# A third accumulating transfer per half, moved loads and a single Block in an attention and FFN kernel

## Chip, cores and metric

One core of one Trainium2 chip. The metric is the device time of one execution in microseconds (us): the median of several runs.

## What is computed

Eight batches of x (512 channels, 1024 positions) go through attention with 16 heads of 32 channels and a key mask, then through a quantised linear layer, and x is added. Cut to what matters:

```python
Q, K, V = proj(Wq), proj(Wk), proj(Wv)                 # einsum 'oc,bct->bto', then 16 heads of 32
att = einsum('bhqd,bhkd->bhqk', Q, K) / sqrt(32) + b
att = softmax(att * m + (1 - m) * NEG_INF)
y = einsum('bhqk,bhkd->bhqd', att, V)                  # back to [B, C, T]
q, in_scale = per_token_quant_int8(y)                  # absmax of a row / 127, rounded
out = einsum('bsk,nk->bsn', q, weight) * in_scale * w_scale + bias
return x + out.astype(float16)
```

## The kernel before

The work has two stages, each in a Block of its own, with a barrier between them.

`project` makes Q, K and V for one batch at a time. Each fp32 operand is split in a high and a low part that TensorE multiplies at its fast rate; the parts of Q and K go to memory (`qk_d`), V too (`v_d`). In the last batch the V products are mixed with the first score maxima of attention. There `w_raw` is the buffer of the raw weights, and `x_hi` and `x_lo` lie in the same memory as `k_stack` and `q_stack`.

`attend` runs 32 steps of four heads. A step has 64 units (`t`), two halves of 512 queries by 8 tiles of 128 keys by 4 heads. In each unit TensorE makes one score block, 128 keys by 512 queries, transposed (`scores`, L724), and half of a row maximum for a coming step (`next_max`, `row_max`, L128), which VectorE reduces (L137). ScalarE takes the exponential into one of eight tiles `probs[:, kt]` (`exps`, L832). At the end of each group of four units `weigh` (L751) adds the previous tile's product with V. Maxima go back into the operands as extra rows: turned on TensorE (L144), split by ScalarE and VectorE (L151, L157), and stored by SyncE (`store_max`, L165) at slot 23 for the second half of the step (units from 32), and at slot 55 for the first half of the next one. The row sums of the softmax are taken at slot 55 (half 0) and, in the next step, at slot 23 (half 1).

The row sum is made in three ways. GpSimd starts DMA transfers that add one whole tile of `probs` (1 MB) onto another (`begin_pair`, L998), two per half: tile 0 onto 1, and 2 onto 3. It adds tiles itself into `acc` (`add`, L1014): 4 and 1, then 3, 5, 6. TensorE adds the rest in `sum_rows`: tile 7 with L763, `acc` with L766. Each tile's slot is free for the next half's exponentials once its reader is through: `FREED` says which add, `READ_BY` which transfer; `exps` waits accordingly. Each engine's order is written out by hand in its `step`; `prev`, `main` and `ahead` say which of the three steps in work take part.

```python
PAIRS_OF_TILES = ((0, 1), (2, 3))
FIRST, ADDED = 4, (1, 3, 5, 6)
...
                for tile in range(first, TT):
                    for h in range(GH):
                        pe.matmul(buf[h * DH:(h + 1) * DH, 0:N], ones[:, :], probs[:, tile, h, :], start=(tile == first), stop=False)
                pe.wait_ge(acc_done, ADDS * halves_before(s, half) + adds)
```

The rest of a step belongs to the step before: GpSimd's `normalise` (L1033) and `finish` (L1039, L1042), VectorE's absmax and scales, the turn of the rounded rows (slot 47) and the product with the weights (`ffn`, L784, slot 51). ScalarE's queue issues the loads between its exponentials (`loads`): K rows at units 0 to 2, bias rows at 4 and 5, V at 8, Q rows at 24 to 26 and 38 to 40, the residual at 30. Row maxima of the next step begin at unit 20 and need its K, bias and Q rows.

Of the kernel before, what the change touches and what calls it, by code (L numbers as in the profile page):

```python
# [25 lines left out]
P = 128  # L26
# [24 lines left out]
PAIRS_OF_TILES = ((0, 1), (2, 3))  # L51
FIRST, ADDED = 4, (1, 3, 5, 6)
# [15 lines left out]
MAX_ROWS = 16 * 2  # L68

# [98 lines left out]
def project(nc, x, mask, wqT, wkT, wvT, qk_d, v_d, bias_d, cond_b, fw, wT, ws_rep, fb_rep, w_scale, f_bias,  # L168
            banks, ring, q_stack, k_stack, neg_max, max_hi, max_lo, ident, v_out, v_stored,
            stack_set, k_loaded, q1_loaded, q2_loaded, rowmax_done, neg_max_done,  # L170
            ident_set, maxT_done, max_hi_done, max_lo_done, max_rows):

    QHI, QLO, KHI, KLO = range(4)
    with ExitStack() as ctx:
        sb = lambda name, shape, dt: ctx.enter_context(nc.sbuf_tensor(name, shape, dt))
        sem = lambda name: ctx.enter_context(nc.semaphore(name))

        w_raw = sb("w_raw", [P, CT, C], F32)
# [25 lines left out]
        proj_done = sem("proj_done")  # L204
# [5 lines left out]
        v_done = sem("v_done")  # L210
        part_stored = [sem(f"part_stored{i}") for i in range(2)]
# [8 lines left out]
        fw_done = sem("fw_done")  # L220
# [5 lines left out]
        GROUPS = 3 * TT  # L226
        V_BANKS = (0, 1, 2)
# [3 lines left out]
        STAGES = 2 * CT  # L231
        block = ctx.enter_context(nc.Block())

        @block.sync
        def _(sp):
# [62 lines left out]
            sp.wait_ge(stack_set, 2)  # L298
            for k in range(3):
                load_q(sp, qk_d, q_stack, 0, 0, 0, k, q1_loaded)  # L300
            for k in range(3):
                load_k(sp, qk_d, k_stack, 0, 0, k, k_loaded)
            for part in range(2):
                load_bias(sp, bias_d, k_stack, 0, 0, part, k_loaded)
            for k in range(3):
                load_q(sp, qk_d, q_stack, 0, 0, 1, k, q2_loaded)
            batch(B - 1, 1, last=True)

            for i in range(2):
                sp.wait_ge(part_stored[i], 32 * B * STAGES // 2)  # L310

        @block.tensor
        def _(pe):
# [13 lines left out]
            def batch(b, par, last=False):  # L327
# [31 lines left out]
                if last:  # L359

                    pe.wait_ge(k_loaded[0], LOADS_K)
# [155 lines left out]
        def _(pool):  # L517
# [11 lines left out]
            def batch(b, par, last=False):  # L529
                if last:  # L530
                    pool.wait_ge(proj_done, GROUPS * b)
                    set_rows(nc, q_stack[0], k_stack[0], stack_set)
                else:
                    split_x(b + 1, 1 - par)
# [16 lines left out]
def attend(nc, x, qk_d, v_d, bias_d, fw, ws_rep, fb_rep, out,  # L551
           banks, ring, q_stack, k_stack, neg_max, max_hi, max_lo, ident, v_out, v_stored,
           stack_set, k_loaded, q1_loaded, q2_loaded, rowmax_done, neg_max_done,
           ident_set, maxT_done, max_hi_done, max_lo_done, max_rows):

    with ExitStack() as ctx:
        sb = lambda name, shape, dt: ctx.enter_context(nc.sbuf_tensor(name, shape, dt))
        sem = lambda name: ctx.enter_context(nc.semaphore(name))

        v_in = sb("v_in", [P, 2, TT, P], F32)  # L560
# [26 lines left out]
        v_loaded = [sem(f"v_loaded{i}") for i in range(2)]  # L587
# [35 lines left out]
        block = ctx.enter_context(nc.Block())  # L623
# [19 lines left out]
        def _(sp):  # L643
            sp.dma_start(v_in[:, 0, :, :], v_d[0]).then_inc(v_loaded[0], 16)

# [33 lines left out]
        def _(pe):  # L679
# [47 lines left out]
            def next_max(s, par, t):  # L727
# [3 lines left out]
                if t % 2 == 0:  # L731
                    if pair == 0:
# [22 lines left out]
            def sum_rows(s, half, buf):  # L755
# [4 lines left out]
                first, adds = (LAST_POOLED, LAST_POOLED - 1) if last else (max(ADDED) + 1, ADDS)  # L760
# [8 lines left out]
            def turn_q(s, buf):  # L769
                if isinstance(s, int) and s == 0:  # L770
                    pe.wait_ge(ident16_set, 1)
                pe.wait_ge(q_done, 2 * s + 2)
# [45 lines left out]
        def _(act):  # L818
# [34 lines left out]
            def loads(s, par, t, prev, ahead):  # L853
# [7 lines left out]
                if ahead and t == 8:  # L861
# [5 lines left out]
                if prev and t == 30:  # L867
                    load_res(s - 1)
                if s == 0 and t == 24:
                    act.wait_ge(stack_set, 4)  # L870
                if ahead and t in (24, 25, 26):
                    load_q(act, qk_d, q_stack, s + 1, 1 - par, 1, t - 24, q2_loaded)
# [27 lines left out]

            for s in range(STEPS + 1):
# [3 lines left out]
        def _(dve):  # L905
            nc.vector.memset(ones[:, :], 1.0).then_inc(const_set, 1)
# [47 lines left out]
            def step(s, par, prev=True, main=True, ahead=True):  # L954
                for t in range(UNITS):
# [30 lines left out]
        def _(pool):  # L986
            set_rows(nc, q_stack[1], k_stack[1], stack_set)
            nc.gpsimd.memset(ident16[:, :], 0.0).then_inc(zeroed, 1)
# [55 lines left out]
            def step(s, par, prev=True, main=True, ahead=True):  # L1044
                if prev and main:
                    add(s - 1, 1, 3)
                if prev:
                    normalise(s - 1, 0)
                if main:
                    for i in range(2):  # L1050
                        begin_pair(s, 0, i)
# [3 lines left out]
                if main:  # L1055
                    for k in range(1, 4):
                        add(s, 0, k)
                if main and ahead:
                    for i in range(2):
                        begin_pair(s, 1, i)  # L1060
# [13 lines left out]
def program(nc, x, mask, wqT, wkT, wvT, cond_b, wT, w_scale, f_bias, out):  # L1074
# [6 lines left out]
    with ExitStack() as ctx:  # L1081
# [9 lines left out]
        v_out = ctx.enter_context(nc.sbuf_tensor("v_out", [P, 2, C], F32))  # L1091
# [38 lines left out]
```

## Time and profile before

| | |
|---|---|
| time, median of 3 runs | 2441.13 us (2439.86 to 2441.28) |
| the profiled execution | 2436.68 us, its span 2434.8 us |
| TensorE matmul busy | 2381.2 us, 98% |
| GpSimd busy | 1673.1 us, 69% |
| VectorE busy | 1560.6 us, 64% |
| ScalarE busy | 1347.4 us, 55% |
| GpSimd's DMA queue (the accumulating transfers) | 132.13 MB, 27.4% of 16 engines' span |
| chain that ended last, TensorE's share | 64% |
| chain that ended last, the stores of `max_lo` | 5% |

Projection ends at about 556 us; from there to the end it is attention. In the tables of the profile a line such as L724 is a line of the kernel before, an arrow gives output and inputs, "idle before" is what the engine stood still ahead of an instruction and who ended that. PE is TensorE, ACT ScalarE, DVE VectorE, POOL GpSimd, SP SyncE; ACTq and SPq are issues of DMAs on their queues.

### The profile page before, as it was taken

Reading aid. Unit: us, or ns where it says so; the run is one execution under the profiler, and the core shown is the slowest. Engines: PE = TensorE matmul, PEld = TensorE weight load, DVE = VectorE, ACT = ScalarE, POOL = GpSimd, SP = SyncE. Lnnn points to the kernel's source line nnn. Section 1 sums busy time; section 2 is a strip of 40 time slices with the busy share of each in tenths; the row PEclk is TensorE's granted clock in tenths of the full one; section 3 lists DMA queues with packets and bytes.
Section 4 is the critical chain, followed back from the end, with each engine's and each line's share of the span. In section 5 each row is a group of like instructions: output and inputs, shape, how many; then the busy total and the mean of one; then the engine's idle time right before and its main releaser. Section 6 shows DMA issues by size and latency. Waiting matters only on the chain.

```text
span 2434.8 us, 37355 instructions
## 1 busy us (share of the span) xinstructions
PE 2381.2 (98%) x12344; PEld 1343.4 (55%) x12376; DVE 1560.6 (64%) x1683; ACT 1347.4 (55%) x2536; POOL 1673.1 (69%) x677
## 2 busy tenths in 40 slices
PE   8999999997999999999999999999999999999996
PEld 7888888884444444444444444444444444444442
DVE  3311111145777787777777777777777777777771
ACT  3322222214666666666666666666666666666664
POOL 3322223414788888888778888887888888888777
PEclk9999999998999999999999999999999999999999
DMA  6655555365677766776777776766776667766751
GB/s 242 255 193 205 211 195 196 149 211 131 149 160 159 159 148 153 161 158 154 156 158 160 156 161 152 159 148 154 158 161 156 153 151 160 159 155 152 157 111 46
DMA packets 143498, 396.55 MB, mean 163 GB/s; under 512 B 14584, under 2 KB 50424, under 8 KB 127296
## 3 DMA queue, kind: packets, MB, share of 16 engines
q0 software_dynamic: 18144, 132.13, 27.4%
q10 hardware_dynamic: 48864, 129.19, 22.0%
q1 hardware_dynamic: 76416, 134.34, 15.1%
q8 instruction: 34, 0.56, 0.1%
q14 instruction: 40, 0.33, 0.0%
HBM read 161.51 MB, written 100.93 MB: 108 GB/s over the span
## 4 chain that ended last, share of the span: by engine, by line
PE 64%; DMA 6%; issue 2%; DVE 2%; POOL 2%; SPq 0%; ACT 0%; ACTq 0%; POOLq 0%; DVEq 0%
PE score L724 21%; PE pv L751 18%; PE ring L128 17%; DMA q_stack<-max_lo 5%; PE ring L784 4%; PE ring L763 2%; PE ring L766 2%; DVE neg_max L137 1%; DMA k_stack<-bias_part 1%; PE ring L775 1%; POOL acc L1014 1%; DMA probs<-probs 0%; PE ring L144 0%; POOL acc L1026 0%; SPq L165 0%
## 5 line engine op out<-in xcount | busy, mean ns | idle before, releaser
L832 ACT ACTIVATE probs<-score 128x512 f32<-128x512 f32 x2048 | 1075.3, 604 | 583.2 <-PE score L724 570.3
L137 DVE TENSOR_REDUCE neg_max<-ring 128x1 f32<-128x1024 f32 x1024 | 1208.6, 1220 | 236.7 <-PE ring L128 225.1
L724 PE MATMUL score<-q_stack,k_stack 100*128 100x512 f32 x2048 | 875.4, 429 | 12.3 <-ACT probs L832 5.5
L1014 POOL TENSOR_TENSOR acc<-acc,probs 128x2048 f32<-128x2048 f32 x189 | 866.9, 4587 | 25.2 <-DMA probs<-probs 10.5
L128 PE MATMUL ring<-k_stack,q_stack 98*128 98x512 f32 x2048 | 810.6, 396 | 12.8 <-DMA k_stack<-bias_part 12.5
L724 PEld LDWEIGHTS score<-q_stack,k_stack 100*128 100x128 f32 x2048 | 387.4, 189 | 492.2 <-ACT probs L832 357.6
L751 PE MATMUL pv<-probs,v_in 128*32 128x512 f32 x4096 | 546.3, 605 | 0.0
L128 PEld LDWEIGHTS ring<-k_stack,q_stack 98*128 98x128 f32 x2048 | 390.7, 191 | 79.1 <-DMA k_stack<-bias_part 12.8
L1014 POOL TENSOR_TENSOR acc<-probs 128x2048 f32<-128x2048 f32 x63 | 289.0, 4588 | 105.0 <-DMA probs<-probs 105.0
L526 POOL TENSOR_TENSOR q_stack<-x_raw,k_stack 128x1024 fp32r<-128x1024 f32 x28 | 67.7, 2455 | 293.1 <-ACT k_stack L402 293.1
L998 POOL DMA_DIRECT2D probs<-probs x126 | 108.7, 863 | 170.2 <-PE pv L751 163.3
L751 PEld LDWEIGHTS pv<-probs,v_in 128*32 128x32 f32 x4096 | 80.6, 108 | 184.8 <-ACT probs L832 162.5
L475 DVE TENSOR_TENSOR part_lo<-score,part_hi 128x512 fp32r<-128x512 f32 x24 | 16.4, 691 | 179.3 <-ACT part_hi L427 179.2
L538 POOL TENSOR_TENSOR part_lo<-k_scaled,part_hi 128x512 fp32r<-128x512 f32 x64 | 82.4, 1307 | 55.1 <-ACT part_hi L430 55.1
L784 PE MATMUL ring<-fw,qT 128*128 128x512 bf16 x480 | 110.0, 382 | 6.2 <-issue 4.9
L1039 POOL TENSOR_TENSOR half<-prod,fb_rep 128x512 f16<-128x512 f32 x64 | 81.5, 1273 | 47.5 <-DVE prod L951 47.5
L325 PE MATMUL ring<-k_stack,w_hi 128*128 128x512 f32 x256 | 101.5, 396 | 0.0
L325 PE MATMUL ring<-q_stack,w_hi 128*128 128x512 f32 x256 | 101.3, 396 | 0.0
L325 PE MATMUL ring<-k_stack,w_lo 128*128 128x512 f32 x256 | 101.2, 395 | 0.0
L430 ACT ACTIVATE part_hi<-k_scaled 128x512 fp32r<-128x512 f32 x64 | 39.0, 628 | 112.1 <-DVE k_scaled L486 83.2
L914 DVE STREAM_TRANSPOSE sums_turned<-ring 128x512 f32<-128x512 f32 x64 | 45.9, 717 | 84.5 <-PE ring L766 84.5
L951 DVE SCALAR_TENSOR_TENSOR prod<-ring,scale,ws_rep 128x512 f32<-128x512 f32 x64 | 48.1, 751 | 80.4 <-PE ring L784 80.4
(101 smaller groups left out, 2028.9 us busy)
## 6 DMA issues: line engine op xcount, KB each, us to landing
probs<-probs POOLq DMA_DIRECT2D x126, 1024.0 KB, 8.0
q_stack<-qk_part ACTq DMA_DIRECT2D x183, 256.0 KB, 4.5
k_stack<-qk_part ACTq DMA_DIRECT2D x90, 512.0 KB
qk_part<-part_hi SPq DMA_DIRECT2D x64, 512.0 KB, 2.6
qk_part<-part_lo SPq DMA_DIRECT2D x64, 512.0 KB, 3.5
v_steps<-v_out SPq DMA_DIRECT2D x64, 256.0 KB, 2.2
v_out<-x ACTq DMA_DIRECT2D x32, 512.0 KB, 5.7
out<-v_out SPq DMA_DIRECT2D x64, 256.0 KB, 2.0
```

Of the source, the lines that this page charges most:

```text
L128: mm = pe.matmul(ring[:, half * N:(half + 1) * N], q_stack[par][0:ROW_MAX, chunk, h, qt * P:(qt + 1) * P], k_stack[par][0:ROW_MAX, h, half ...
L137: nc.vector.tensor_reduce(neg_max[:, pair // CHUNK, pair % CHUNK:pair % CHUNK + 1], ring[:, :], AX_X, ALU.max, negate=True).then_inc(neg_m ...
L325: return pe.matmul(bank[:, :], lhsT, rhs, start=(k == 0), stop=(k == 3 * CT - 1))
L526: nc.gpsimd.tensor_tensor(x_lo[par][:, a, :], x_raw[:, a, :], x_hi[par][:, a, :].bitcast(F32), ALU.subtract).then_inc(x_lo_done, 1)
L538: nc.gpsimd.tensor_tensor(part_lo[:, g % 2, th * N:(th + 1) * N], k_scaled[:, i % 2, :], part_hi[:, g % 2, th * N:(th + 1) * N].bitcast(F3 ...
L724: pe.matmul(score[score_bank(t)][:, :], k_stack[par][0:ROWS, h, kt * P:(kt + 1) * P], q_stack[par][0:ROWS, half, h, :], start=True, stop=T ...
L751: mm = pe.matmul(pv[h * DH:(h + 1) * DH, :], v_in[:, par, kt % TT, h * DH:(h + 1) * DH], probs[:, kt % RING, h, :], start=(kt % TT == 0), ...
L784: mm = pe.matmul(buf[:, cols], qT[:, tt, :], fw[:, tt, cols], start=(tt == 0), stop=(tt == TT - 1))
L832: nc.scalar.activation(probs[:, kt, h, :], score[score_bank(t)][:, :], ACT.Exp).then_inc(exp_done, 1)
L998: pool.dma_start(probs[:, b, :, :], probs[:, a, :, :], accum_op=ALU.add).then_inc(pair_done[i], 16)
L1014: nc.gpsimd.tensor_tensor(acc[:, half, :, :], first, probs[:, tile, :, :], ALU.add).then_inc(acc_done, 1)
L1039: nc.gpsimd.tensor_tensor(half16[:, half, :], prod[:, half, :], fb_rep[:, cols], ALU.add).then_inc(half_done, 1)
```

## The change

A third transfer per half adds tile 6 onto tile 5; GpSimd's adds take tiles 1, 3, 7, 5; `acc` then holds all eight tiles, and TensorE's sum has no term from `probs` except in the very last half. The third transfer waits for the weigh of tile 5 and the exponentials of tile 6. GpSimd's order of issues, adds and finishes is new. On ScalarE's queue V moves to unit 16, the residual to 22, the second half of Q to 33, 34 and 36. VectorE takes absmax of half 0 at slot 27. The two stages share one Block, with waits in place of the barrier; `v_in` lies outside the stages and serves as `w_raw` before; V of step 0 is loaded from the first stage; the constant rows 96 to 99 of the stacks are set alone (K first), and only the bias loads wait for them.

```diff
-PAIRS_OF_TILES = ((0, 1), (2, 3))
-FIRST, ADDED = 4, (1, 3, 5, 6)
+PAIRS_OF_TILES = ((0, 1), (2, 3), (6, 5))
+FIRST, ADDED = 4, (1, 3, 7, 5)
...
-    nc.gpsimd.memset(q_stack[:, :, :, :].bitcast(F32), LIFT).then_inc(stack_set, 1)
-    nc.gpsimd.memset(k_stack[:, :, :].bitcast(F32), 1.0).then_inc(stack_set, 1)
+    nc.gpsimd.memset(k_stack[ROW_BIAS:ROWS, :, :].bitcast(F32), 1.0).then_inc(stack_set, 1)
+    nc.gpsimd.memset(q_stack[ROW_BIAS:ROWS, :, :, :].bitcast(F32), LIFT).then_inc(stack_set, 1)
...
-        w_raw = sb("w_raw", [P, CT, C], F32)
+        w_raw = v_in[:, :, :, :].rearrange("p i a c -> p (i a c)").rearrange("p (a c) -> p a c", a=CT)
...
-        V_BANKS = (0, 1, 2)
+        V_BANKS = tuple((bank + SCORES - TT) % SCORES for bank in range(SCORES))
...
-            sp.wait_ge(stack_set, 2)
+            sp.wait_ge(proj_done, GROUPS * (B - 1))
             for k in range(3):
                 load_q(sp, qk_d, q_stack, 0, 0, 0, k, q1_loaded)
             for k in range(3):
                 load_k(sp, qk_d, k_stack, 0, 0, k, k_loaded)
+            sp.wait_ge(stack_set, 1)
             for part in range(2):
                 load_bias(sp, bias_d, k_stack, 0, 0, part, k_loaded)
             for k in range(3):
                 load_q(sp, qk_d, q_stack, 0, 0, 1, k, q2_loaded)
+            sp.wait_ge(fw_done, 1)
+            for i in range(2):
+                sp.wait_ge(v_stored[i], 16 * (B - 1) * TT // 2)
+            sp.dma_start(v_in[:, 0, :, :], v_d[0]).then_inc(v_loaded[0], 16)
             batch(B - 1, 1, last=True)
...
-        block = ctx.enter_context(nc.Block())
...
-            sp.wait_ge(stack_set, 4)
+            sp.wait_ge(proj_done, PROJECTED)
             for k in range(3):
                 load_q(sp, qk_d, q_stack, 1, 1, 0, k, q1_loaded)
             for k in range(3):
                 load_k(sp, qk_d, k_stack, 1, 1, k, k_loaded)
+            sp.wait_ge(stack_set, 3)
             for part in range(2):
                 load_bias(sp, bias_d, k_stack, 1, 1, part, k_loaded)
...
+                if isinstance(s, int) and s == 0 and t < SCORES:
+                    pe.wait_ge(v_done, B * TT - SCORES + 1 + t)
...
-                first, adds = (LAST_POOLED, LAST_POOLED - 1) if last else (max(ADDED) + 1, ADDS)
+                first, adds = (LAST_POOLED, LAST_POOLED - 1) if last else (TT, ADDS)
...
-                if ahead and t == 8:
+                if ahead and t == 16:
...
-                if prev and t == 30:
+                if prev and t == 22:
                     load_res(s - 1)
...
-                if ahead and t in (24, 25, 26):
-                    load_q(act, qk_d, q_stack, s + 1, 1 - par, 1, t - 24, q2_loaded)
+                if ahead and t in (33, 34, 36):
+                    load_q(act, qk_d, q_stack, s + 1, 1 - par, 1, (33, 34, 36).index(t), q2_loaded)
...
+            for i in range(2):
+                act.wait_ge(part_stored[i], 16 * B * STAGES)
...
-                    if t == 19 and prev:
-                        take_absmax(s - 1, 0)
-                        take_floor(s - 1)
...
                     if t == SUMS_1 + 4 and prev:
                         spread(s - 1, 1)
+                        take_absmax(s - 1, 0)
+                        take_floor(s - 1)
...
                 pool.wait_ge(pv_done, QH * TT * s + half * TT + b + 1)
+                if a > b:
+                    pool.wait_ge(exp_done, UNITS * s + GH * (half * TT + a + 1))
...
                 if prev and main:
+                    begin_pair(s, 0, 0)
                     add(s - 1, 1, 3)
+                elif main:
+                    begin_pair(s, 0, 0)
                 if prev:
                     normalise(s - 1, 0)
                 if main:
-                    for i in range(2):
-                        begin_pair(s, 0, i)
+                    begin_pair(s, 0, 1)
                     add(s, 0, 0)
                 if prev:
                     normalise(s - 1, 1)
                 if main:
+                    begin_pair(s, 0, 2)
                     for k in range(1, 4):
                         add(s, 0, k)
                 if main and ahead:
-                    for i in range(2):
-                        begin_pair(s, 1, i)
+                    begin_pair(s, 1, 0)
+                    begin_pair(s, 1, 1)
+                    add(s, 1, 0)
...
                 if prev:
-                    for half in range(2):
-                        finish(s - 1, half)
+                    finish(s - 1, 0)
                 if main and ahead:
-                    for k in range(3):
+                    begin_pair(s, 1, 2)
+                if prev:
+                    finish(s - 1, 1)
+                if main and ahead:
+                    for k in range(1, 3):
                         add(s, 1, k)
```

## Rows read from the trace of the kernel before

**Rows 1.** Busy time of each engine in eight steps: length, PE, PEld, DVE, ACT, POOL, clock, DMA, GB/s.

```profile
668.50:1129.01 460.51, 457.86 (x2504) 225.64 (x2512) 362.22 (x385) 298.56 (x576) 378.63 (x144) 1.00 0.71 156
```

**Rows 2.** Groups by line, window of one step, 1129.01 to 1186.61: count, busy us, mean ns, idle.

```profile
L763 PE MATMUL ring<-probs,ones 128*32 128x512 f32 x16 | 2.1, 605 | 0.0
```

**Rows 3.** Chain that ended last: the product L784; timeline of TensorE at slot 55.

```profile
1129.01 3.40 PE ring L784 x15
1186.61 3.40 PE ring L784 x15
...
1135.22 0.28 PE L144 MATMUL ring<-ident,neg_max 128*16 128x128 f32 x1
1135.43 1.06 PE L763 MATMUL ring<-probs,ones 128*32 128x512 f32 x8
1136.31 1.04 PE L766 MATMUL ring<-acc,ones 128*32 128x512 f32 x8
1137.29 0.50 PE L724 MATMUL score<-q_stack,k_stack 100*128 100x512 f32 x1
1140.34 0.50 PE L724 MATMUL score<-q_stack,k_stack 100*128 100x512 f32 x1
```

**Rows 4.** Timeline of GpSimd (POOL) over one step: start, length, instruction, idle before.

```profile
1141.27 13.92 POOL L1014 TENSOR_TENSOR acc<-acc,probs 128x2048 f32<-128x2048 f32 x3
1156.37 0.87 POOL L998 DMA_DIRECT2D probs<-probs  x1
1159.35 0.85 POOL L998 DMA_DIRECT2D probs<-probs  x1 [2.11 <-PE pv L751]
1163.48 4.58 POOL L1014 TENSOR_TENSOR acc<-probs 128x2048 f32<-128x2048 f32 x1 [3.28 <-DMA probs<-probs]
1168.06 1.29 POOL L1033 TENSOR_TENSOR y<-y_raw,factor 128x512 f32<-128x512 f32 x1
1169.74 13.92 POOL L1014 TENSOR_TENSOR acc<-acc,probs 128x2048 f32<-128x2048 f32 x3 [0.38 <-DMA probs<-probs]
1189.16 1.27 POOL L1039 TENSOR_TENSOR half<-prod,fb_rep 128x512 f16<-128x512 f32 x1 [1.24 <-DVE prod L951]
1191.63 1.28 POOL L1039 TENSOR_TENSOR half<-prod,fb_rep 128x512 f16<-128x512 f32 x1
```

**Rows 5.** Chain at 1163, then landing of `max_lo` stores issued at 1136.75 (tile view).

```profile
1163.25 7.01 DMA q_stack<-max_lo
1170.38 0.50 PE score L724
...
DMA to landing us min/median/max: 1.8/1.8/1.8
```

**Rows 6.** Tile `probs`, landing of the transfers issued at 1156.37 and at 1159.35.

```profile
DMA to landing us min/median/max: 6.9/6.9/6.9
DMA to landing us min/median/max: 10.2/10.2/10.2
```

**Rows 7.** Stretches of one step: columns as in rows 1, DMA share is next to last.

```profile
1145.00:1155.60 10.60, 10.60 (x59) 5.03 (x57) 8.51 (x8) 7.98 (x16) 10.44 (x4) 1.00 0.95 201
1157.60:1162.90 5.30, 5.30 (x38) 2.22 (x41) 4.95 (x7) 3.02 (x7) 0.85 (x1) 1.00 1.07 219
1162.90:1173.70 10.80, 10.67 (x61) 4.91 (x54) 8.46 (x9) 6.42 (x13) 9.83 (x3) 1.00 0.98 209
1185.00:1194.40 9.40, 9.24 (x58) 3.84 (x58) 6.06 (x7) 3.34 (x8) 5.94 (x6) 1.00 1.07 221
```

**Rows 8.** The seam: timeline at 557, SyncE's loads, chain, and two stretches as in rows 1.

```profile
557.70 0.47 PE L724 MATMUL score<-q_stack,k_stack 100*128 100x512 f32 x1 [1.60 <-PEq L174]
564.66 1.29 SPq L103 DMA_DIRECT2D q_stack<-qk_part  x3
568.24 18.08 DMA k_stack<-bias_part
573.90:586.30 12.40, 0.00 (x0) 0.00 (x0) 0.01 (x1) 0.60 (x1) 5.20 (x2) 0.59 1.03 236
586.30:593.30 7.00, 6.93 (x20) 3.85 (x21) 2.73 (x3) 2.73 (x6) 6.22 (x3) 0.51 0.01 2
```

More of the change, by code:

```diff
@@ L68 @@
 MAX_ROWS = 16 * 2
+GROUPS = 3 * TT
+STAGES = 2 * CT
+PROJECTED = GROUPS * B
 def wait(eng, sem, value):
@@ L203, in project @@
         x_lo_done = sem("x_lo_done")
-        proj_done = sem("proj_done")
         q_hi_done = sem("q_hi_done")
@@ L209, in project @@
         k_lo_done = sem("k_lo_done")
-        v_done = sem("v_done")
-        part_stored = [sem(f"part_stored{i}") for i in range(2)]
         small_loaded = sem("small_loaded")
@@ L359, in batch @@
                 if last:
+                    pe.wait_ge(stack_set, 2)
                     pe.wait_ge(k_loaded[0], LOADS_K)
@@ L531, in batch @@
                     pool.wait_ge(proj_done, GROUPS * b)
+                    pool.wait_ge(k_lo_done, TT * b)
                     set_rows(nc, q_stack[0], k_stack[0], stack_set)
+                    pool.wait_ge(stack_set, 2)
                 else:
@@ L586, in attend @@
         zeroed = sem("zeroed")
-        v_loaded = [sem(f"v_loaded{i}") for i in range(2)]
         res_loaded = sem("res_loaded")
@@ L621, in ring_of @@
             return ring[(len(USES) * par + PLACE[use]) % 2]
-        block = ctx.enter_context(nc.Block())
         def all_steps(eng, body):
@@ L731, in next_max @@
                 if t % 2 == 0:
+                    if isinstance(own, int) and (own, pair) == (1, 0):
+                        pe.wait_ge(stack_set, 4)
                     if pair == 0:
@@ L771, in turn_q @@
                     pe.wait_ge(ident16_set, 1)
+                    pe.wait_ge(fw_done, 1)
                 pe.wait_ge(q_done, 2 * s + 2)
@@ L905, in _ @@
         def _(dve):
+            dve.wait_ge(proj_done, PROJECTED)
+            for i in range(2):
+                dve.wait_ge(part_stored[i], 16 * B * STAGES)
             nc.vector.memset(ones[:, :], 1.0).then_inc(const_set, 1)
@@ L986, in _ @@
         def _(pool):
+            pool.wait_ge(proj_done, PROJECTED)
+            for i in range(2):
+                pool.wait_ge(part_stored[i], 16 * B * STAGES)
             set_rows(nc, q_stack[1], k_stack[1], stack_set)
+            pool.wait_ge(stack_set, 4)
             nc.gpsimd.memset(ident16[:, :], 0.0).then_inc(zeroed, 1)
@@ L1058, in step @@
                 if main and ahead:
-                    for i in range(2):
-                        begin_pair(s, 1, i)
+                    begin_pair(s, 1, 0)
+                    begin_pair(s, 1, 1)
+                    add(s, 1, 0)
                 if main and not ahead:
@@ L1095, in program @@
         banks = score + [buf[:, half * N:(half + 1) * N] for buf in ring for half in range(2)] + [pv]
-        stack_set, rowmax_done, neg_max_done, ident_set, maxT_done, max_hi_done, max_lo_done = (
+        stack_set, rowmax_done, neg_max_done, ident_set, maxT_done, max_hi_done, max_lo_done, proj_done, v_done, fw_done = (
             ctx.enter_context(nc.semaphore(name)) for name in
-            ("stack_set", "rowmax_done", "neg_max_done", "ident_set", "maxT_done", "max_hi_done", "max_lo_done"))
-        k_loaded, q1_loaded, q2_loaded, max_rows, v_stored = (
+            ("stack_set", "rowmax_done", "neg_max_done", "ident_set", "maxT_done", "max_hi_done", "max_lo_done",
+             "proj_done", "v_done", "fw_done"))
+        k_loaded, q1_loaded, q2_loaded, max_rows, v_stored, v_loaded, part_stored = (
             [ctx.enter_context(nc.semaphore(f"{name}{i}")) for i in range(2)]
-            for name in ("k_loaded", "q1_loaded", "q2_loaded", "max_rows", "v_stored"))
+            for name in ("k_loaded", "q1_loaded", "q2_loaded", "max_rows", "v_stored", "v_loaded", "part_stored"))
+        sems = ctx.enter_context(ExitStack())
+        block = ctx.enter_context(nc.Block())
         shared = (banks, ring, q_stack, k_stack, neg_max, max_hi, max_lo, ident, v_out, v_stored,
                   stack_set, k_loaded, q1_loaded, q2_loaded, rowmax_done, neg_max_done,
-                  ident_set, maxT_done, max_hi_done, max_lo_done, max_rows)
+                  ident_set, maxT_done, max_hi_done, max_lo_done, max_rows,
+                  block, sems, v_in, v_loaded, proj_done, part_stored, v_done, fw_done)
         project(nc, x, mask, wqT, wkT, wvT, qk_d, v_d, bias_d, cond_b, fw, wT, ws_rep, fb_rep, w_scale, f_bias, *shared)
```

19 lines of the change are left out of this document (7 added, 12 removed).

## The prediction

> **What bounds the kernel now.** I read the stretches of the run first. Behind the first projection and attention steps TensorE is busy 457.9 of 460.5 us at its full clock, while VectorE, ScalarE and GpSimd have gaps [rows 1]; so in the 32 attention steps TensorE's own instructions set the pace. Next the start of the same feed-forward product in consecutive steps: 1129.01 and 1186.61, one step is 57.6 us [rows 3]. Four score units with their maxima and one weigh take 3.05 us, from 1137.29 to 1140.34 [rows 3]; the rest of a step is the two row sums, the turn of q and the product. Then what is nearly late. The rows of the maxima that unit 32 needs are stored while an accumulating transfer is in flight; the store lands 7.0 us after its issue, and the next score starts 0.12 us later: no slack [rows 5]. The same store at slot 55, with the transfers over, lands in 1.8 us [rows 5]. GpSimd is third: 378.6 of 460.5 us busy [rows 1].
>
> I count a step from its unit 0 (here 1143.4, two groups of four behind 1137.29). Now unit 20 comes at 15.3, slot 23's sum from 18.3 to 20.4, unit 32 at 26.5.
>
> **The sum term that goes.** One half's sum is L763 at 1135.43, L766 at 1136.31, the next score at 1137.29 [rows 3]. L763, the term of tile 7, takes 16 instructions a step [rows 2], 8 a half; it holds TensorE for 1136.31 - 1135.43 = 0.88 us. It goes in 63 of 64 halves (the last half keeps its tiles): 63 x 0.88 = 55.4 us, all on the path. A step would be 57.6 - 1.76 = 55.8 us, unit 32 comes at 25.6. The number of GpSimd adds stays: tile 7 takes the place of tile 6, and 6 goes onto 5 in a transfer.
>
> **The third transfer, on the DMA engines.** A lone transfer lands 6.9 us after its issue, one issued 3 us behind another 10.2 us [rows 6]; the engines are full for about 5.3 us of it [rows 7]. Two more a step are 10.6 us. Full or nearly so are now 10.6 us (K rows and V), 5.3 and 10.8 us (two transfers, Q rows, residual), 9.4 us (two transfers) [rows 7], and some 6 us of Q loads and stores beside: about 42 of 57.6. It becomes 52 of 55.8. The total fits; each transfer can be in the way of something with a deadline.
>
> **The third transfer, on GpSimd.** An add takes 13.92 / 3 = 4.64 us, an issue 0.86, a normalise 1.29, one finish 1191.63 - 1189.16 = 2.47 [rows 4]. From issue to the add that waits for it is 1163.48 - 1156.37 = 7.1 us [rows 4]. The new order puts all four adds of half 1, both finishes and three issues in a ring that closes through TensorE. The last add now takes tile 5, and unit 20's exponential overwrites that slot, where before the last add freed tile 6, needed a group later. The exponential can be some 0.6 us late behind score 20 at 15.8 (my estimate: three score banks at 0.47 us each, less the exponential), so the last add must end by 16.4. From there: to the factor for the second normalise 7.4 us (it starts at 1168.06, 24.7 behind unit 0 [rows 4], less 0.88); normalise 1.3; issue 0.9; three adds 13.9; the first transfer of half 1, issue to add, 7.1 (its add stands ahead of the finishes that covered it); its add 4.6; finish, issue, finish 5.8; two adds 9.3; issue and last add 5.5. Sum 55.8 us. So GpSimd's ring is as long as TensorE's step. It costs nothing only if no transfer lands later than the lone one.
>
> **The moved loads and what they meet.** V goes from unit 8 to 16, the residual from 30 to 22, the second Q half from 24 to 33, all on ScalarE's queue; the issue instructions are the same. Away from unit 24 the Q loads no longer compete with the maxima. But V (issued at 12.5) now meets the first transfer of the half (issued at about 10.9, engines to 17.4), and with the residual (issued at 17.2) it stands before the second transfer (issued at 17.7, engines from 19.2). Each is 512 KB; at 201 GB/s [rows 7] 2.6 us each. So the second transfer ends between 24.3 (it goes ahead) and 27.5 (it waits for both), against 24.3 needed by the ring with 1.1 us to spare. The stores of the maxima, issued at 19.9, land some 2 us behind the end of that transfer, as now: 26 to 29 against unit 32 at 25.6. A late score relaxes the ring, so the transfer moves ahead again, by as much as the score is late; the two share the loss. Bounds for both together: 0 (all lands as the lone one) and 2.1 us a step (27.5 less 24.3, less the spare 1.1). I take 0.7, nearest to the present margin of 0.12 us less the 0.88 that TensorE gains on the store: 31 x 0.7 = 22 us. Absmax of half 0, moved from VectorE's slot 19 to 27, waits for a normalise that is through by then; slot 35 uses it; nothing. The K rows, 1.57 MB from unit 0, need 1.57 / 0.201 = 7.8 us of engines; the new transfer of half 1 (issued at about 54.3, engines to about 4.9 of the next step) holds them to 12.7, and unit 20 reads them at 15.3: nothing, with 2.6 us of cover. If that cover goes: third rival.
>
> A rule of the Trainium skill speaks against this loss: "DMA: Bandwidth & Descriptors", Queues, rings and completion order, has each engine take turns between the rows of queues packet by packet. By that, the small store would pass a transfer. The 7.0 us of one store beside 1.8 of the other [rows 5] do not agree. By the rule the sum would lose nothing in the steps; that is the first rival.
>
> **The seam between the stages.** One Block in place of two, rows 96 to 99 set alone, K and Q rows of step 1 loaded ahead of the sets. Now TensorE idles 1.6 us at the Block's end, ahead of 557.70 [rows 8], then 12.4 us (573.9 to 586.3, nothing executed), released by a K bias load issued behind the Q and K loads of 564.66 that lands 18 us later; behind that stall 7.0 us run at 0.51 of the clock, its lower level, 1.2 GHz [rows 8]. At full clock these 20 instructions need about half, 3.5 us less. Together 1.6 + 12.4 + 3.5 = 17.5 us, and about 1 for a slow stretch behind the first idle time. The loads start at about 558 instead of 564.66; TensorE's need moves 1.6 us ahead; so 5 of the 12.4 are certain, and the bias then also goes ahead of both transfers for the most part, whose 10.6 us were what it waited for. I take 14 us of the 18.5; bounds 5 (only the shift of the loads) and 19. The new waits: SyncE waits for stores of V and the table ahead of its V load, with the K parts of the last batch queued behind; a store takes 2 us or so and TensorE has none of it; ScalarE, VectorE and GpSimd wait for the last stores of the parts, done long before. Nothing. The last step's GpSimd chain keeps its length; -1 to +2 us, taken at 0.
>
> **Sum.** 55.4 - 22 + 14 = 47.4 us. The profiled execution took 2436.7 us (span 2434.8), the median is 2441.1, 4.4 us above: 2436.7 - 47.4 + 4.4 = 2393.7. I say 2393.
>
> **Rivals.**
> 1. *TensorE alone sets the pace.* All transfers land as lone ones do, and the store slips between: 55.4 + 15.7 gained, 2370 us. For it: the ring closes at 55.8 as well, and the transfers of a half no longer come as a pair. Against: four near ties would all have to fall well, and one that has 0.12 us now. Chance 0.23.
> 2. *GpSimd's ring or the DMA engines take the place of TensorE* at about 57.4 us a step, 1.5 lost and more: 31 x 0.2 + 14 gained, 2421 us. For it: a ring without slack, 94% of DMA time in use. Against: a lone transfer's 6.9 us has little spread where nothing is beside it. Chance 0.22.
> 3. *Slower: the K rows land behind unit 20.* If the first transfer of half 0 (engines from 12.3) gets ahead of the last of the K rows, these wait until 17.4 and land at about 18.3: 3.0 us lost in each of 30 steps, against 1.76 gained: +37 - 14 = +23, 2464 us. It decides once the K rows end later than 12.3, now reckoned at 12.7 with packets of both mixed; against it speaks that a load under way has not been cut off in the steps. Chance 0.12.
> 4. *The seam gives nothing* (the stall moves to the new transfer): 2407 us, within my range; it is part of the others.
>
> **How the numbers follow.** The forecast, 56.2 to 56.9 us a step, has 0.43 and by itself 2380 to 2410. The range 2366 to 2430 takes in rivals 1 and 2, stops short of the upper bound of 2.1 us a step in every step (2437 us), and leaves out the third. Measurement tells 0.2%, 5 us, from no change. Faster: 0.43 + 0.23 + most of 0.22, 0.84; within 0.2%: 0.04, the upper end of rival 2; slower: 0.12.
>
> **What would show it.** L763 at 32 instructions, those of the last half. Feed-forward products 56.5 us apart; 55.8 is rival 1, 57.4 rival 2, over 58 rival 3. Score L724 waiting for max_lo in most steps, 0.3 to 1 us each; exponentials L832 waiting for the last add at unit 20; if instead the ring kernel L128 waits for K rows, it is rival 3. GpSimd without idle time but for the first transfer of half 1, some 5 us. The seam: no stall over 4 us at about 572. I am wrong if loads and transfers shared the engines without holding each other up, or if one transfer of three lands later than 8 us in all steps.

## The result and the profile after

| | before | changed |
|---|---|---|
| median, timed side by side | 2440.49 us | 2414.22 us (2413.03 to 2418.17) |
| profiled execution, its span | 2436.68, 2434.8 us | 2414.74, 2412.8 us |
| GpSimd's DMA queue | 132.13 MB, 27.4% | 198.19 MB, 42.9% |

The ratio is 0.9898, 95% interval 0.9882 to 0.9913: faster by 1.0%. The forecast was 2393, in a range from 2366 to 2430. The measured gain is 26 us where 47 were forecast: the sign held, and a little over half of the size.

The same stretch of eight and a bit steps as in [rows 1], in the changed kernel (length; busy time of PE, PEld, DVE, ACT, POOL; clock; DMA share; GB/s), then the chain that ended last at two feed-forward products, which answer to [rows 3], and the one sum of `probs` that is left on TensorE:

```profile
653.63:1120.00 466.37, 456.15 (x2416) 224.06 (x2423) 366.99 (x390) 299.71 (x581) 394.73 (x162) 1.00 0.89 194
...
1112.81 3.40 PE ring L788 x15
1169.84 3.40 PE ring L788 x15
...
L766 PE MATMUL ring<-probs,ones 128*32 128x512 f32 x32 | 3.6, 592 | 0.0
```

TensorE now stands still 10.2 of 466.4 us, where it was 2.7 of 460.5. The DMA share is 0.89 where it was 0.71. The sum term is gone but for the last half's 32 instructions. A step takes 57.0 us here, 57.3 in the mean, where 56.5 was forecast.

Where a step's time goes can be read off the timeline by the starts of the 64 score products. I took, for the 27 steps 3 to 29, the gap behind each unit less the shortest gap ever seen at that unit in the profiled kernels with three transfers (for those with two, the shortest in the kernel before at slots 23 and 55); the sum of the shortest gaps is the step without any wait. Mean per step in us:

| kernel | step | without waits | units 0-7 | 19-23 | 29-31 | others |
|---|---|---|---|---|---|---|
| before | 57.58 | 56.76 | 0.04 | 0.02 | 0.42 | 0.34 |
| changed | 57.28 | 55.03 | 0.68 | 0.50 | 0.65 | 0.42 |

So the removed term gives 56.76 - 55.03 = 1.73 us a step, as forecast (1.76), and the waits, 2.25 us where they were 0.82, take 1.43 of it back. They have grown at three places. First units 0 to 7; ScalarE's timeline there, then the issues of its K loads over the whole run (min, median, max in ns) in the changed kernel:

```profile
1127.00 1.63 ACTq L113 DMA_DIRECT2D k_stack<-qk_part  x2
1127.46 0.59 ACT L836 ACTIVATE probs<-score 128x512 f32<-128x512 f32 x1
1128.68 0.60 ACT L836 ACTIVATE probs<-score 128x512 f32<-128x512 f32 x1 [0.62 <-PE score L725]
1128.69 1.23 ACTq L113 DMA_DIRECT2D k_stack<-qk_part  x1
1129.97 0.60 ACT L836 ACTIVATE probs<-score 128x512 f32<-128x512 f32 x1 [0.69 <-PE score L725]
1130.18 1.06 ACTq L119 DMA_DIRECT2D k_stack<-bias_part  x1
...
L113 ACTq DMA_DIRECT2D k_stack<-qk_part x90: 317/1220/1272, 611.4 to 2273.2; - x90
```

and the same issues in the kernel before:

```profile
L110 ACTq DMA_DIRECT2D k_stack<-qk_part x90: 317/419/565, 626.4 to 2296.6; - x90
```

The third transfer of half 1 is in flight at the start of a step. The first of the three K issues takes 0.32 us in both kernels, the second and the third about 1.24 us where they took 0.42 (medians of steps 3 to 29); over all 90 the median went from 0.42 to 1.22. The exponential behind a long issue starts late: 1128.68, 1.2 us behind the one before. The reader should note that the profile puts the gap down to TensorE ("<-PE score"); TensorE had itself waited for a score bank that this ScalarE had not emptied. The chain of waits of the changed kernel names the true one:

```profile
1128.68 0.60 ACT probs L836
1129.27 0.65 ACTq L113
1130.18 0.87 ACTq L119
1131.05 0.50 ACT probs L836
```

Second, units 19 to 23 and, third, 29 to 31; who waited for whom between 700 and 2300 us (total us, times, longest), and one such wait in TensorE's timeline:

```profile
ACT probs L836 <- POOL acc L1026: 25.5, 15, 3.0
PE score L725 <- DMA q_stack<-max_lo: 16.7, 27, 1.5
PEld score L725 <- DMA q_stack<-max_lo: 3.8, 2, 2.4
...
1153.60 0.50 PE L725 MATMUL score<-q_stack,k_stack 100*128 100x512 f32 x1 [0.59 <-DMA q_stack<-max_lo]
```

The exponentials of unit 20 wait for GpSimd's last add in 15 of 28 steps, up to 3.0 us; unit 32 waits for the store of the maxima in nearly every one, 29 waits of 20.5 us in all, where the same view of the kernel before has 14 of 5.7 us. GpSimd's order in that step, to be held beside [rows 4]:

```profile
1124.96 0.86 POOL L1010 DMA_DIRECT2D probs<-probs  x1
1128.33 9.24 POOL L1026 TENSOR_TENSOR acc<-acc,probs 128x2048 f32<-128x2048 f32 x2
1137.74 0.89 POOL L1010 DMA_DIRECT2D probs<-probs  x1 [0.17 <-issue]
1138.35 4.89 POOL L1026 TENSOR_TENSOR acc<-acc,probs 128x2048 f32<-128x2048 f32 x1
1144.12 1.19 POOL L1010 DMA_DIRECT2D probs<-probs  x1
```

From 1124.96 to 1144.12 it has hardly a gap; its last add ends at 1143.2, 16.8 us behind the step's unit 0 at 1126.4 (16.4 was the latest that costs nothing by the prediction).

The seam, to be held beside [rows 8]: GpSimd's two sets of four rows (as long as those of 128 rows), SyncE's loads, and a stretch in which the kernel before stood still for 12.4 us:

```profile
557.40 3.52 POOL L124 MEMSET k_stack<- 4x4096 f32 x1 [30.19 <-PE score L324]
558.42 1.48 SPq L106 DMA_DIRECT2D q_stack<-qk_part  x3
559.94 1.38 SPq L113 DMA_DIRECT2D k_stack<-qk_part  x3
561.37 1.24 SPq L119 DMA_DIRECT2D k_stack<-bias_part  x2
...
560.00:600.00 40.00, 38.16 (x195) 19.19 (x194) 29.16 (x26) 26.45 (x51) 27.20 (x13) 1.00 0.91 199
```

The set of 128 rows in the kernel before, at 557.66, took 3.52 us too. TensorE is busy 38.2 of 40 us at its full clock of 2.4 GHz.

### The profile page after: what moved, and what is told of

Same layout as the page of the kernel before. It is cut to its first block, busy times and chain, and to the rows that moved or that the text cites. A ratio compares the mean times of both kernels' runs of the same rounds, so it can differ in the third digit from the quotient of the medians.

```text
span 2412.8 us, 36511 instructions
## 1 busy us (share of the span) xinstructions
PE 2342.3 (97%) x11840; PEld 1320.4 (55%) x11872; DVE 1561.4 (65%) x1683; ACT 1343.3 (56%) x2536; POOL 1725.1 (71%) x740
## 3 DMA queue, kind: packets, MB, share of 16 engines
q0 software_dynamic: 27216, 198.19, 42.9%
q10 hardware_dynamic: 48864, 129.19, 20.5%
## 4 chain that ended last, share of the span: by engine, by line
PE 77%; DMA 10%; POOL 5%; issue 3%; ACT 2%; ACTq 1%; SPq 1%; DVE 1%; POOLq 0%; DVEq 0%
PE score L725 18%; PE pv L754 16%; PE ring L131 15%; PE ring L324 11%; PE score L324 9%; DMA q_stack<-max_lo 8%; PE ring L788 4%; POOL acc L1026 4%; PE pv L324 3%; PE ring L769 1%; ACT probs L836 1%; DMA k_stack<-bias_part 1%; ACTq L119 1%; DMA probs<-probs 1%; PE ring L779 1%
## 5 line engine op out<-in xcount | busy, mean ns | idle before, releaser
L1026 POOL TENSOR_TENSOR acc<-acc,probs 128x2048 f32<-128x2048 f32 x189 | 876.8, 4639 | 21.5 <-DMA probs<-probs 12.9
L1010 POOL DMA_DIRECT2D probs<-probs x189 | 172.8, 914 | 52.2 <-PE pv L754 48.8
L475 DVE TENSOR_TENSOR part_lo<-score,part_hi 128x512 fp32r<-128x512 f32 x24 | 16.4, 691 | 179.1 <-ACT part_hi L427 179.1
L1051 POOL TENSOR_TENSOR half<-prod,fb_rep 128x512 f16<-128x512 f32 x64 | 90.5, 1415 | 10.4 <-DVE prod L958 10.4
L788 PEld LDWEIGHTS ring<-fw,qT 128*128 128x128 bf16 x512 | 48.0, 99 | 81.7 <-DVE neg_max L140 25.2
```

The source lines that it names most:

```text
L788: mm = pe.matmul(buf[:, cols], qT[:, tt, :], fw[:, tt, cols], start=(tt == 0), stop=(tt == TT - 1))
L1010: pool.dma_start(probs[:, b, :, :], probs[:, a, :, :], accum_op=ALU.add).then_inc(pair_done[i], 16)
L1026: nc.gpsimd.tensor_tensor(acc[:, half, :, :], first, probs[:, tile, :, :], ALU.add).then_inc(acc_done, 1)
L1051: nc.gpsimd.tensor_tensor(half16[:, half, :], prod[:, half, :], fb_rep[:, cols], ALU.add).then_inc(half_done, 1)
```

## Experiments

My theory: three waits, each with its own cause (A, ScalarE held by its own load issues; B, GpSimd's ring through unit 20; C, the maxima's store behind the second transfer), took the gain. The rival: the DMA engines, 0.89 busy, set the pace, so that a wait taken away comes back elsewhere.

The changed kernel was timed in the first session alone, where the kernel before had 2440.49 us; beside the experiments the kernel before had 2436.8 to 2437.5. A difference of 3 us or so from 2414.22 is therefore no difference; the ratio to the kernel before (0.9898 for the changed one) is the safer measure, and the step is the mean of one profiled execution.

**The seam alone.** Edit on the changed kernel: steps, transfers and loads as before (its first lines).

```diff
-PAIRS_OF_TILES = ((0, 1), (2, 3), (6, 5))
-FIRST, ADDED = 4, (1, 3, 7, 5)
+PAIRS_OF_TILES = ((0, 1), (2, 3))
+FIRST, ADDED = 4, (1, 3, 5, 6)
...
```

> The changed kernel with its steps put back as before (two transfers per half, tile 7 summed on TensorE, old order of loads and of GpSimd); only the single Block, the constant rows and the early loads of step 1 stay. My theory: the seam is worth 13 to 14 us by itself (first feed-forward product 14.9 us earlier, of which 1.8 are sum terms), so 2427 us. Rival: most of that is the sums and the third transfer's order in the first steps, the seam is worth 5 us, 2436 us.

2424.05 us against 2436.93 of the kernel before: 0.9947 (0.9930 to 0.9963), 12.9 us. The seam is worth that; what is left of the change, 1.0% less 0.5%, is the steps.

**A quarter of the third transfer.**

```diff
-                pool.dma_start(probs[:, b, :, :], probs[:, a, :, :], accum_op=ALU.add).then_inc(pair_done[i], 16)
+                heads = slice(0, 1) if a > b else slice(0, GH)
+                pool.dma_start(probs[:, b, heads, :], probs[:, a, heads, :], accum_op=ALU.add).then_inc(pair_done[i], 16)
```

> The third transfer adds only one of the four heads of tile 6 onto tile 5 (256 KB instead of 1 MB), so the row sums leave out three heads of tile 6; every instruction and wait is kept. Theory of three waits (ScalarE held by its own load issues at units 0 to 5, GpSimd's last add late for unit 20, the stores of the maxima late for unit 32), of which the first and the third come from the DMA engines being held: the first wait (0.65 us a step) goes, the others shrink, 56.1 us a step, 2380 us. Rival, GpSimd's ring alone sets the pace: its adds and issues are unchanged, only a wait for a landing can go, 57.0 us a step or 2405 us.

2397.60 us, 0.9835 (0.9819 to 0.9851), step 56.65: between the two. The second and third K issues take 0.45 and 0.42 us again, and units 0 to 7 lose 0.05 us instead of 0.68; units 19 to 23 lose 0.45, and 29 to 31 0.69, both as in the changed kernel. A is due to the third transfer's bytes; B and C are not, which I had wrong for C.

**Tile 7 last.**

```diff
-FIRST, ADDED = 4, (1, 3, 7, 5)
+FIRST, ADDED = 4, (1, 3, 5, 7)
```

> One line: GpSimd adds tiles 1, 3, 5, 7 instead of 1, 3, 7, 5, so the slot of tile 5 comes free one add (4.6 us) earlier and the last add frees tile 7, needed at unit 28. Three-waits theory: the wait of the exponentials at unit 20 for the last add (0.48 us a step in the changed kernel) goes, 14 us less, 2400 us. Rival, the DMA engines (89% busy) set the pace: the wait comes back as another one and the time stays within 4 us of 2414.

2674.01 us, 1.0980 (1.0957 to 1.1002), 65.7 us a step: far outside both. GpSimd's timeline in this kernel:

```profile
1136.19 0.87 POOL L1010 DMA_DIRECT2D probs<-probs  x1
1139.57 4.58 POOL L1026 TENSOR_TENSOR acc<-acc,probs 128x2048 f32<-128x2048 f32 x1
1149.94 4.53 POOL L1026 TENSOR_TENSOR acc<-acc,probs 128x2048 f32<-128x2048 f32 x1 [5.79 <-DMA probs<-probs]
```

The add of tile 5 needs the third transfer. As third add it stands there 13.7 us behind the issue, with K rows issued at 1135.23 in the same engines; as fourth, the add of tile 7 covers that. I had looked at which slot comes free and not at what the add itself waits for. From the add at 1098.14 to the same one at 1164.39, GpSimd waits four times for a landing and hardly for anything else: 3.5 + 5.4 + 5.8 + 2.5 = 17.2 us, with some 48.5 us of work (see the next experiment) the 65.7 of the step. TensorE, held so, also loses its clock:

```profile
1155.20 0.80 PE L725 MATMUL score<-q_stack,k_stack 100*128 100x512 f32 x1 [3.68 <-ACT probs L836]
...
1155.00:1165.00 10.00, 8.53 (x27) 3.48 (x27) 3.62 (x5) 3.69 (x8) 7.49 (x5) 0.50 0.96 206
```

Behind 3.7 us without work its granted clock is 0.50, the lower level of 1.2 GHz. In this step GpSimd never waits for TensorE, so the clock comes with the loss and is not its cause; over the whole run its share was not taken apart.

**Tile 7 last and K rows on SyncE.** The line above and the edit of the next experiment.

> Tile 7 last, as the one line that cost 260 us, and K and bias rows on SyncE's queue, that is issued some 2.5 us later, behind the output stores. If the 13.6 us from issue to landing of the third transfer came from the K rows standing ahead of it in the DMA engines, it now goes first, lands in 7 to 9 us, and the kernel is back at 2400 to 2415 us. If GpSimd cannot use tile 5 as its third add in any case (the ring is too long with that wait in it), it stays above 2600 us.

2547.94 us, 1.0448 (1.0431 to 1.0466), 61.3 us a step: again outside both. The wait of half 1 is gone, the ones of half 0 and of the first transfer of half 1 are not:

```profile
1112.75 9.26 POOL L1026 TENSOR_TENSOR acc<-acc,probs 128x2048 f32<-128x2048 f32 x2
...
1132.62 4.57 POOL L1026 TENSOR_TENSOR acc<-probs 128x2048 f32<-128x2048 f32 x1 [3.22 <-DMA probs<-probs]
...
1147.75 9.25 POOL L1026 TENSOR_TENSOR acc<-acc,probs 128x2048 f32<-128x2048 f32 x2 [3.16 <-DMA probs<-probs]
...
1164.07 4.60 POOL L1026 TENSOR_TENSOR acc<-probs 128x2048 f32<-128x2048 f32 x1 [5.38 <-DMA probs<-probs]
```

3.2 + 3.2 + 5.4 us of waits and some 48.5 us of work (394.73 of 466.37 us are GpSimd's in the changed kernel, 57.3 us a step) are 60.3 of the step's 61.3 us: the ring is full, and each wait for a landing in it costs its whole length. So of the 260 us that tile 7 last cost, K rows ahead of the transfer were 126; the rest is this.

**K and bias rows on SyncE's queue.**

```diff
-                if s > 0 and ahead and t < 3:
-                    if t == 0:
-                        wait(act, score_done, UNITS * s)
-                    load_k(act, qk_d, k_stack, s + 1, 1 - par, t, k_loaded)
-                if s > 0 and ahead and t in (4, 5):
-                    load_bias(act, bias_d, k_stack, s + 1, 1 - par, t - 4, k_loaded)
...
+                if prev and ahead:
+                    sp.wait_ge(score_done, UNITS * s)
+                    for k in range(3):
+                        load_k(sp, qk_d, k_stack, s + 1, 1 - par, k, k_loaded)
+                    for part in range(2):
+                        load_bias(sp, bias_d, k_stack, s + 1, 1 - par, part, k_loaded)
```

> K and bias rows of the coming step are issued on SyncE's queue, behind the output stores, instead of on ScalarE's at units 0 to 5; otherwise the changed kernel. Three-waits theory: ScalarE no longer stands behind its own issues while the third transfer holds the DMA engines, 0.65 us a step less, 2394 us, or 2404 if the last add then is late by what TensorE gained. Rival, DMA engines set the pace: within 4 us of 2414. If the K rows come too late by this, TensorE waits for them at unit 20 and the kernel is slower than 2414.

2410.96 us, 0.9888 (0.9872 to 0.9905): not to be told from the changed kernel. Yet the waits moved: units 0 to 7 from 0.68 to 0.04 us, units 19 to 23 from 0.50 to 0.98. In this kernel, from 700 to 2300 us:

```profile
ACT probs L842 <- POOL acc L1026: 43.1, 23, 3.5
```

A went, and in the mean B took three quarters of it. But more than a third of B's 0.98 is in three early steps (3 to 5, the last two with some TensorE time below full clock: 0.97 and 0.94 in 784 to 843 and 843 to 905 us); what starts that is open. In steps 6 to 29 B grows from 0.42 to 0.69, four tenths of what A gave, and the step falls from 57.23 to 56.83. By itself the total fits the rival; the place fits the ring.

**The first transfer of half 1 ahead of the last add of half 0.**

```diff
                     begin_pair(s, 0, 2)
-                    for k in range(1, 4):
+                    for k in range(1, 3):
                         add(s, 0, k)
                 if main and ahead:
                     begin_pair(s, 1, 0)
+                if main:
+                    add(s, 0, 3)
+                if main and ahead:
                     begin_pair(s, 1, 1)
```

> GpSimd issues the first transfer of half 1 ahead of its last add of half 0 instead of behind it, so its flight (7.1 us) lies beside that add (4.64 us). Ring theory (GpSimd's ring closes through unit 20 and sets the step together with TensorE's waits): the ring is some 3.7 us shorter, until the second transfer's wait for the weigh of tile 11 holds it; the wait at unit 20 (0.48 us a step) goes, and the second transfer of half 0 goes out earlier, so the maxima's store lands earlier too (0.63 less a part); 56.4 us a step, 2390 us. Rival, DMA engines at 89% set the pace: the transfer now meets the Q loads of units 33 to 40, and the time stays at 2410 or above.

2412.98 us, 0.9904 (0.9887 to 0.9921): my 2390 was wrong, and the total is the rival's. Units 19 to 23 lose 0.04 us instead of 0.50, so B was the ring; units 29 to 31 lose 1.06 instead of 0.65. The store of the maxima lands 27.3 us behind unit 0, in the changed kernel 27.1 (medians, steps 3 to 29): it stays where it was, and unit 32, no longer held at unit 20, waits for it longer.

**Both**: the last edit and K and bias rows on SyncE.

> Both: the first transfer of half 1 ahead of the last add of half 0, and K and bias rows on SyncE's queue. K on SyncE alone took away ScalarE's 0.65 us a step, and 0.45 of it came back at unit 20, as the ring theory says. With the ring shorter it should not come back: 0.65 + 0.48 less than 57.28, and a part of the maxima's 0.63: 55.9 us a step, 2375 us, well below both kernels. Rival (DMA engines): within 5 us of K on SyncE alone, 2411.

2374.87 us, 0.9749 (0.9733 to 0.9766), as the theory of three waits says. The DMA engines do the same transfers and loads as in the changed kernel, in 39 us less: they did not set the pace, and the rival falls. The store now lands 25.9 us behind unit 0.

**Only the residual back at unit 30.**

```diff
-                if prev and t == 22:
+                if prev and t == 30:
```

> The changed kernel with only the residual's load back at unit 30. Theory of three waits that stand in for each other: the wait for the maxima's store at unit 32 (0.65 us a step) goes, since the residual no longer stands before the second transfer and the store; but GpSimd's ring is not shorter, so most of it comes back at unit 20: 57.1 us a step, 2409 us. If waits simply add up: 56.65 us a step, 2395 us.

2401.83 us, 0.9858 (0.9842 to 0.9875), between the two: units 29 to 31 lose 0.10 instead of 0.65. Units 19 to 23 lose less too, 0.30, against what I expected, and the other places 0.29 more together. The second transfer lands 8.6 us behind its issue instead of 9.9, the store 5.7 instead of 6.3 (medians, steps 3 to 29). So what C costs in the changed kernel is the residual that stands before the second transfer and the store.

**The early transfer and the residual at 30**, K rows on ScalarE.

> The first transfer of half 1 ahead of the last add, and the residual at unit 30; K and bias rows stay on ScalarE's queue. Alone the early transfer moved 0.46 us from unit 20 to unit 32 and gained nothing. With the residual out of the way unit 32 should not take it up: only ScalarE's wait at units 0 to 7 (0.7 us) is left, 56.4 us a step, 2388 us. If the third wait grows instead (K rows late at unit 20), 57 us and 2408.

2385.74 us, 0.9790 (0.9774 to 0.9806): only ScalarE's 0.77 us at units 0 to 7 is left.

**All three**: early transfer, K and bias rows on SyncE, residual at 30.

> As the one before, with the residual's load back at unit 30. If the residual at unit 22 is what stands before the second transfer and so before the maxima's stores (0.63 us a step), this is 10 to 15 us less than the one before. If the wait at unit 32 comes from the second transfer alone, which the small stores cannot pass, no change (within 4 us); if the residual then meets the Q loads of 33 to 40 and the third transfer, it is slower.

2366.89 us, 0.9714 (0.9698 to 0.9730): 70 us less than the kernel before and some 45 less than the changed one. It is 8 us less than with the first two edits alone, between my 10 to 15 and the 4 that would have been no change. The same waits as above, 700 to 2300 us:

```profile
ACT probs L842 <- POOL acc L1026: 9.4, 7, 2.3
PEld score L731 <- DMA q_stack<-max_lo: 2.4, 2, 1.5
PE score L731 <- DMA q_stack<-max_lo: 0.8, 2, 0.6
```

**All loads of ScalarE back, with three transfers.**

```diff
-                if ahead and t == 16:
+                if ahead and t == 8:
...
-                if prev and t == 22:
+                if prev and t == 30:
...
-                if ahead and t in (33, 34, 36):
+                if ahead and t in (24, 25, 26):
```

> The changed kernel with only the loads on ScalarE's queue put back (V at unit 8, residual at 30, second Q half at 24 to 26). If the moves are what lets the third transfer fit: V at unit 8 stands behind the K rows, that stand behind the third transfer, and reaches into the first transfer of half 0; the Q loads meet the stores of the maxima; 58 us a step or more, above 2435 us. If the moves are worth nothing: 57.2 us, 2414 us. The prediction's own view, that V and the residual hold up the second transfer at their new places, would give less time than 2414.

2440.06 us, 1.0009 (0.9999 to 1.0018): no gain is left. Units 29 to 31 lose 1.20 us with the residual at 30 as well, so C has other causes than the residual: the store lands 27.8 us behind unit 0 here. The kernel with only the residual back differs from this one in V and the second half of Q alone, and takes 2401.83: those two moves are worth 38 us. Which of them was not tried.

**A control: two transfers, K rows on SyncE.**

> Two transfers a half as in the kernel before, single Block, K and bias rows on SyncE's queue. A control: with no third transfer in flight at the step's start ScalarE's issues are not held (0.04 us a step lost at units 0 to 7), so moving them should be worth nothing: 2424 us, 57.5 us a step. If the move is worth something by itself, it is below 2419 and part of the gain of the combined version is not owed to the third transfer's cost.

2424.76 us, 0.9952 (0.9935 to 0.9968), the same as the seam alone. Moving the K rows is worth something only where a third transfer holds ScalarE's issues. A page of the Trainium skill, "Trainium Kernel Development and Optimization", Key Constraints, says that issuing from several engines only saves the sequencer's issue time, since all run on the same DMA engines. The trace agrees that the issue time is what moved: on SyncE the K issues of this control have a median of 0.38 us, and of 1.01 us in the kernel with a third transfer, where ScalarE's had 1.22.

All kernels with their waits, in us a step, read as above:

| kernel | time | step | units 0-7 | 19-23 | 29-31 | others |
|---|---|---|---|---|---|---|
| changed | 2414.2 | 57.28 | 0.68 | 0.50 | 0.65 | 0.42 |
| quarter of the third | 2397.6 | 56.65 | 0.05 | 0.45 | 0.69 | 0.43 |
| K on SyncE | 2411.0 | 57.08 | 0.04 | 0.98 | 0.66 | 0.38 |
| early transfer | 2413.0 | 57.26 | 0.74 | 0.04 | 1.06 | 0.40 |
| residual at 30 | 2401.8 | 56.82 | 0.77 | 0.30 | 0.10 | 0.62 |
| early, K on SyncE | 2374.9 | 55.96 | 0.04 | 0.07 | 0.46 | 0.37 |
| early, residual at 30 | 2385.7 | 56.39 | 0.77 | 0.05 | 0.02 | 0.51 |
| all three | 2366.9 | 55.73 | 0.04 | 0.11 | 0.04 | 0.53 |
| loads back | 2440.1 | 57.91 | 0.65 | 0.67 | 1.20 | 0.36 |

## Why the prediction was right and where it missed

The sign and the range held and the point was 21 us too low. That 2414 lies in the range is in part luck: the range was made for waits at units 20 and 32, and the largest of the three waits had no term in it.

- **The sum term**, 55.4 us: 63 halves x 1.73 / 2 = 54.5 us. Right.
- **The waits in the steps**, 22 us: this is the term that was mis-sized. They are 1.43 us a step, 44 us. The two that the prediction named, the last add at unit 20 (0.48 more than before) and the maxima's store (0.23 more), make 0.71 together, against 0.7 taken. That agreement is partly luck: it holds with ScalarE's wait beside them, which hides some of theirs (with K rows on SyncE they make 1.20). The third it did not have: 0.64 us a step, 20 us, is ScalarE behind its own issues. The steps that failed are the sentences "the issue instructions are the same" and, of the K rows, "nothing": I asked when the rows would land and not how long the engine that issues them is held. With these 20 us the forecast would have been 2413; that it is so near 2414 is luck too, by the smaller misses below.
- **GpSimd's ring** closing through unit 20: the place is right, and shown by the early transfer, which emptied it. The length of 55.8 us was never measured free of other waits; with ScalarE's wait gone, steps 6 to 29 take 56.8. One term of it does not follow from its own numbers: three banks at 0.47 us less an exponential of 0.60 are 0.8 us, not 0.6, which makes 55.6.
- **The sign "one transfer of three lands later than 8 us in all steps"** came true. From issue to landing the three of half 0 take 9.2, 9.9 and 8.5 us, those of half 1 6.9, 9.4 and 9.0 (medians, steps 3 to 29; those of half 0 never under 8.3). The prediction should have named which of them the ring waits for: the first of half 1 does land as a lone one, and the others lie mostly beside adds. The second of half 0 lands 27.5 us behind unit 0, the upper bound, and GpSimd waits 0.4 us a step for it.
- **The residual before the second transfer and the store**: right (0.46 us a step, 12 us against 2414.22, by its own run). **V at 16 as a cost**: not borne out; V and the second Q half moved together are worth 38 us. I worked out what the moved loads meet at their new places and never what they would have met, beside a third transfer, at their old ones.
- **The first rival's small store that passes a transfer**, which the prediction takes from the Trainium skill ("DMA: Bandwidth & Descriptors", Queues, rings and completion order): in the changed kernel the second transfer is issued at 1144.12 and lands at 1153.7; the store issued at 1147.17 lands at 1153.5, 6.3 us later, near the 7.0 of [rows 5] and far from the 1.8 of a free one. It waited for nearly the whole transfer.
- **The seam**, 14 us: 12.9. Right. The tail, taken at 0: from the start of the last product to the end it is 13.1 us instead of 11.0, a loss of 2 us. The terms as measured, 54.5 - 44 + 12.9 - 2 = 21 us, are what the two profiled executions show (21.9); the medians are 26.3 apart.
- **The rivals.** Rival 2, a step of 57.4, came nearest in its time (2421), but of its two reasons the DMA engines fall with the two combined kernels; the ring is borne out in part, by the wait at unit 20. Rival 3, the slower one, did not come: TensorE waited 1.8 us in all for bias rows.

## What to carry to other kernels

In a kernel where several engines are near their limit, waits stand in for each other: K rows on SyncE and the early transfer each gave nothing that the timing can tell (3 and 1 us), both together 39 us. So read the loss by its place in the step, not only by the total, before an edit is thrown away. Of a large DMA that is added, ask three things: who issues while it flies, what small DMA with a deadline is queued behind it, and what loads at their old places it meets; and of a reordered add, ask first what it waits for.

## What the runs showed of the hardware

- Issuing a load takes longer while a 1 MB accumulating transfer runs: 1.22 us median beside 0.42 for the same K load on ScalarE's queue, and with the K rows on SyncE's queue it is SyncE that is held (1.01 us beside 0.38 with two transfers). With a quarter of the bytes the median is back at 0.42. I had taken an issue as a fixed cost.
- Such a transfer landed 6.8 to 6.9 us after its issue at the least, and 13.6 us after it in the kernel with tile 7 last, with three K loads of 512 KB issued in the 1 us before it.
- An 8 KB store issued 3 us behind such a transfer landed 6.3 us later, 0.3 us before it; 1.8 us with none in flight.
- In the kernel with tile 7 last TensorE stood still for 3.7 us, and from 1155 to 1165 us, behind it, its granted clock was 0.50.
- Setting 4 rows of 4096 values takes GpSimd 3.52 us, the same as 128 rows.
